# Two bounds of a clipped scan: filled apart on TensorE instead of one widened in place

## The reference

```python
Ad = 1.0 + dt * A                      # (batch, token, 16), just around 1
Bd = Bm * min(norm(xn), 1.0)
def step(h, inputs):
    ad, bd, xt, ct = inputs
    h = clip(h * ad[:, :, None] + bd[:, :, None] * xt[:, None, :], -10.0, 10.0)
    yt = einsum('bd,bdh->bh', ct, h)
    return (h, yt)
```

## Time and profile before

| what | value |
|---|---|
| time, median of 3 runs | 2083.74 us (2082.17 to 2084.46) |
| the profiled execution's own time | 2086.27 us |
| its span in the trace | 2084.4 us, 46452 instructions |
| PE busy | 1916.6 us, 92% |
| POOL busy | 1747.5 us, 84% |
| DVE busy | 1603.2 us, 77% |
| ACT busy | 1377.9 us, 66% |
| TensorE's granted clock, mean | 0.985 of full speed |

### The profile page before, as it was taken

The page is one execution under the profiler, slowest core; times in us unless marked ns, Lnnn a source line. Parts: engine busy times, 40 slices in busy tenths (PEclk is TensorE's granted clock), DMA queues, the critical chain, the costliest instruction groups (busy, mean ns, idle before and its releaser), DMA issues.

```text
span 2084.4 us, 46452 instructions
## 1 busy us (share of the span) xinstructions
PE 1916.6 (92%) x16624; PEld 1441.5 (69%) x16624; DVE 1603.2 (77%) x2045; ACT 1377.9 (66%) x3462; POOL 1747.5 (84%) x1444
## 2 busy tenths in 40 slices
PE   5589999999999999999999999999999999999988
PEld 5467776776776776776677777676777677777665
DVE  3377887878887877887787887787887787887786
ACT  4577666677666667766676766776766676766643
POOL 1388888889888889888889988889988888988886
PEclk9699999999999999999999999999999999999999
DMA  5121212121212121212121112221112121121110
GB/s 175 57 63 44 63 48 63 56 68 44 62 47 63 56 68 49 58 47 63 56 68 52 56 46 64 58 65 53 56 48 64 56 64 57 53 58 53 55 54 16
DMA packets 98437, 122.37 MB, mean 59 GB/s; under 512 B 31072, under 2 KB 68336, under 8 KB 93536
## 3 DMA queue, kind: packets, MB, share of 16 engines
q1 hardware_dynamic: 98208, 119.41, 20.1%
HBM read 62.07 MB, written 9.31 MB: 34 GB/s over the span
## 4 chain that ended last, share of the span: by engine, by line
PE 50%; ACT 18%; issue 15%; DVE 12%; POOL 2%; SPq 2%; DMA 1%; DVEq 0%; ACTq 0%; POOLq 0%
PE ps_y L588 10%; DVE ks L981 7%; PE ps_job L465 7%; PE ps_job L503 7%; PE ps_fill L561 6%; PE ps_fill L552 5%; PE ps_job L478 4%; ACT low L786 4%; ACT tap L744 3%; PE ps_y L568 3%; PE ps_job L472 2%; ACT xh L682 2%; ACT lend L764 1%; ACT gate L676 1%; DVE pf L932 1%
## 5 line engine op out<-in xcount | busy, mean ns | idle before, releaser
L1079 POOL TENSOR_TENSOR prod<-ks,crep 128x512 f32<-128x512 f32 x1024 | 1286.7, 1276 | 159.0 <-DVE ks L981 153.4
L981 DVE TENSOR_TENSOR_SCAN ks<-low,ps_fill 128x512 f32<-128x512 f32 x1024 | 1208.1, 1208 | 255.4 <-PE ps_fill L561 251.6
L786 ACT COPY low<-ps_fill 128x512 f32<-128x512 f32 x1024 | 585.1, 581 | 534.3 <-PE ps_fill L552 534.2
L588 PE MATMUL ps_y<-c_sb,prod 128*128 128x128 f32 x4096 | 610.9, 274 | 2.2 <-POOL prod L1079 1.4
L588 PEld LDWEIGHTS ps_y<-c_sb,prod 128*128 128x128 f32 x4096 | 459.3, 142 | 80.2 <-issue 43.4
L561 PE MATMUL ps_fill<-spans,pick 128*128 128x512 f16 x1024 | 390.3, 381 | 61.8 <-ACT low L786 51.8
L552 PEld LDWEIGHTS ps_fill<-ts,xs 128*128 128x128 f16 x4096 | 315.2, 98 | 174.5 <-issue 8.5
L552 PE MATMUL ps_fill<-ts,xs 128*128 128x128 f16 x4096 | 397.4, 220 | 11.8 <-DVE ks L981 6.0
L744 ACT ACTIVATE tap<-xr,cols_sb 128x128 f32<-128x128 f32 x768 | 251.7, 392 | 0.0
L460 PE MATMUL ps_job<-x,w_in 128*128 128x128 f16 x3072 | 216.5, 222 | 10.3 <-POOL x L1049 7.8
L465 PE MATMUL ps_job<-w_in,x 128*128 128x512 f16 x768 | 203.2, 381 | 21.3 <-ACT gate L676 21.3
(11 more groups left out here) (123 smaller groups left out, 2063.8 us busy)
## 6 DMA issues: line engine op xcount, KB each, us to landing
crep<-c_dram SPq DMA_DIRECT2D x32, 1024.0 KB, 4.8
xs<-xh SPq DMA_DIRECT2D x256, 64.0 KB, 2.0
xs<-xl SPq DMA_DIRECT2D x224, 64.0 KB, 2.0
xf<-in_xT SPq DMA_DIRECT2D x32, 256.0 KB, 2.8
res<-in_x SPq DMA_DIRECT2D x32, 256.0 KB, 2.6
out_dram<-res SPq DMA_DIRECT2D x32, 256.0 KB, 2.1
ts<-tth SPq DMA_DIRECT2D x128, 32.0 KB
ts<-tth SPq DMA_DIRECT2D x128, 31.0 KB
```

Source lines behind the costliest of these rows:

```text
L588: last = mm(ps_y[:, cut], prod[:, (TILES * k + s) % HOLD, e, :], ident, start=False, stop=(u % 4 == 3 and q == 3 and e == QN - 1), is_tran ...
L786: copy(low[:, (TILES * k + s) % RING], ps_fill[:, (TILES * k + s) % RING]).then_inc(sem["low_copied"], 1)
L981: nc.vector.tensor_tensor_scan(ks[:, u % 2, QN * q:QN * (q + 1)].rearrange("d n t -> d (n t)"), low[:, g % RING], ps_fill[:, g % RING], 0. ...
L1079: tt(prod[:, g % HOLD], ks[:, u % 2, part], crep[:, p, part], ALU.mult).then_inc(sem["weighed"], 1)
```

## The change

Each tile's two bounds are made by two fills of the same form. Lower bounds go to two banks (`LOWS`), upper bounds to three (`HIGHS`). The upper fill uses the same weights `xs` and a row stack of its own, `ts[:, p, 1]`, which differs from the lower one in rows 0 and 32 alone (+10/p in place of -10/p). The matmul `widen` with `spans` and `pick` goes. PE runs, in step s, the lower fill of tile s+3 and the upper fill of tile s+2. The slots in `low` become four (`LOWRING`), and ACT's copy now waits for the scan of the tile four back. DVE's scan waits for the copy and for the upper fill.

On SP the stack DMAs run for both row stacks, one stack after the other, so twenty-four in place of twelve; the bounds take four DMAs out and four back in place of three and three; the constant rows of `ts` are loaded four times at the start in place of twice. Two large memsets at the start go. The core of the diff:

```diff
-RING = 5
-AHEAD = 3
+LOWS = 2
+HIGHS = 3
+LOWRING = 4
+AHEAD = (3, 2)
...
-        ts = sb("ts", [P, 2, NSUB, NS * SUB], H)
+        ts = sb("ts", [P, 2, 2, NSUB, NS * SUB], H)
...
-        N_STACK = 16 * (3 * NSUB + NSUB - 1)
-        N_BOUND = 16 * 3
+        N_STACK = 16 * (6 * NSUB + NSUB - 1)
+        N_BOUND = 16 * 4
...
-                    loads.append((ts[96:128, p], carry))
+                    for v in range(2):
+                        loads.append((ts[96:128, p, v], carry))
...
-                    sp.dma_start(r_dram.rearrange("h n t -> n h t"), bnd16[:, :, 1]).then_inc(sem["bound_out"], 16)
...
-                    for jj in range(NSUB):
-                        a = SUB * jj
-                        for r, half in ((0, tth), (SUB, ttl), (2 * SUB, tth)):
+                    for v in range(2):
+                        for jj in range(NSUB):
+                            a = SUB * jj
+                            for r, half in ((0, tth), (SUB, ttl), (2 * SUB, tth)):
+
+                                lead = 0 if r == 2 * SUB else 1
+                                sp.dma_start(ts[r + lead:r + SUB, pn, v, jj],
+                                             half[a + lead:a + SUB].rearrange("s n t -> s (n t)")).then_inc(stack, 16)
...
-            def fill(k, p, s):
+            def fill(k, p, s, v):
...
-                if s == 0:
+                if s == 0 and v == 0:
...
-                since(pe, "scanned", g - RING + 1)
-                o = ps_fill[:, g % RING].rearrange("d (n t) -> d n t", n=QN)
+                if v == 0:
+                    since(pe, "low_copied", g - LOWS + 1)
+                else:
+                    since(pe, "scanned", g - HIGHS + 1)
+                o = ps_fill[:, (g % LOWS, LOWS + g % HIGHS)[v]].rearrange("d (n t) -> d n t", n=QN)
...
-            def widen(k, p, s):
-
-                q = s % NQ
-                pe.wait_ge(sem["low_copied"], TILES * k + s + 1)
-                mm(ps_fill[:, (TILES * k + s) % RING], pick[:], spans[:, p, q * BANK:(q + 1) * BANK], start=False, stop=True,
-                   skip_group_check=True).then_inc(sem["bounded"], 1)
...
+                    ahead(k, p, s + AHEAD[0], 0)
+                    ahead(k, p, s + AHEAD[1], 1)
...
-                    for v, clip in enumerate((-CLIP, 2 * CLIP)):
+                    for v, clip in enumerate((-CLIP, CLIP)):
...
+                    act.wait_ge(sem["low_filled"], TILES * k + s + 1)
+                    since(act, "scanned", TILES * k + s + 1 - LOWRING)
+                    copy(low[:, (TILES * k + s) % LOWRING], ps_fill[:, (TILES * k + s) % LOWS]).then_inc(sem["low_copied"], 1)
...
-                    dve.wait_ge(sem["bounded"], g + 1)
+                    dve.wait_ge(sem["low_copied"], g + 1)
+                    dve.wait_ge(sem["high_filled"], g + 1)
```

More of the change, by code:

```diff
@@ L73 @@
 gw_ready wdt_ready wdt_set sums_ready sums_taken halo_set prep prepared act_prep
-filled low_copied bounded scanned weighed flipped
+low_filled high_filled low_copied scanned weighed flipped
 xr_ready xr_taken xt_ready xt_taken z_ready z_taken zT_ready zT_high zT_taken
@@ L170, in build @@
         xs = sb("xs", [P, 2, NSUB, DI], H)
-        ts = sb("ts", [P, 2, NSUB, NS * SUB], H)
-        low = sb("low", [P, RING, BANK])
+        ts = sb("ts", [P, 2, 2, NSUB, NS * SUB], H)
+        low = sb("low", [P, LOWRING, BANK])
         ks = sb("ks", [P, 2, NS, P])
@@ L333, in body @@
                     xstack, stack = sem[f"xstack_in{pn}"], sem[f"stack_in{pn}"]
-                    since(sp, "filled", TILES * k)
+                    since(sp, "low_filled", TILES * k)
+                    since(sp, "high_filled", TILES * k)
                     sp.wait_ge(sem["xn_done"], j + 1)
@@ L362, in body @@
                     sp.wait_ge(sem["bound_all"], j + 1)
[L363 to L366, removed]
-                    sp.dma_start(r_dram.rearrange("h n t -> n h t"), bnd16[:, :, 1]).then_inc(sem["bound_out"], 16)
+                    for v, bound in enumerate((scratch, r_dram)):
+                        for h in range(2):
+                            sp.dma_start(bound[h].rearrange("j n t -> n j t"),
+                                         bnd16[:, h, v].rearrange("n (j t) -> n j t", j=NSUB)
+                                         ).then_inc(sem["bound_out"], 16)
                     sp.wait_ge(sem["c_out"], 16 * (j + 1))
@@ L375, in body @@
                                      ).then_inc(sem[f"ones_in{pn}"], 16)
[L376 to L383, removed]
-                    sp.wait_ge(sem["tt_done"], 2 * (j + 1))
-                    for jj in range(NSUB):
-                        a = SUB * jj
-                        for r, half in ((0, tth), (SUB, ttl), (2 * SUB, tth)):
-                            lead = 0 if r == 2 * SUB else 1
-                            sp.dma_start(ts[r + lead:r + SUB, pn, jj],
-                                         half[a + lead:a + SUB].rearrange("s n t -> s (n t)")).then_inc(stack, 16)
+                    sp.wait_ge(sem["bound_out"], 64 * (j + 1))
+                    for v, bound in enumerate((scratch, r_dram)):
+                        for h in range(2):
+                            sp.dma_start(ts[SUB * h:SUB * h + 1, pn, v].rearrange("o j c -> o (j c)"),
+                                         bound[h].rearrange("(o j) n t -> o (j n t)", o=1)
+                                         ).then_inc(sem[f"bound_in{pn}"], 16)
+                    sp.wait_ge(sem["tt_done"], 2 * (j + 1))
+                    for v in range(2):
[5 more added lines that the diff above has]
+                                             half[a + lead:a + SUB].rearrange("s n t -> s (n t)")).then_inc(stack, 16)
                     sp.wait_ge(sem["lend_set"], 2 * j + 2)
@@ L620, in body, with ahead @@
                     jobs_at(k, p, 2 * s + 1)
+            def ahead(k, p, s, v):
+                if s < TILES and exists(k, 0):
+                    fill(k, p, s, v)
+                elif s >= TILES and exists(k, 1):
+                    fill(k + 1, 1 - p, s - TILES, v)
             steps(body)
@@ L719, in side @@
                     since(act, "bound_all", k + 1)
-                    since(act, "bound_out", 48 * (k + 1))
-                    for v, clip in enumerate((-CLIP, 2 * CLIP)):
+                    since(act, "bound_out", 64 * (k + 1))
+                    for v, clip in enumerate((-CLIP, CLIP)):
                         act_fn(ad[:, v], pf[:, 0], ACT.Identity, scale=clip).then_inc(sem["bound32"], 1)
@@ L784, in copy_low @@
                 def copy_low(k, s):
-                    act.wait_ge(sem["filled"], TILES * k + s + 1)
-                    copy(low[:, (TILES * k + s) % RING], ps_fill[:, (TILES * k + s) % RING]).then_inc(sem["low_copied"], 1)
+                    act.wait_ge(sem["low_filled"], TILES * k + s + 1)
+                    since(act, "scanned", TILES * k + s + 1 - LOWRING)
+                    copy(low[:, (TILES * k + s) % LOWRING], ps_fill[:, (TILES * k + s) % LOWS]).then_inc(sem["low_copied"], 1)
                 for s in range(TILES):
[L789 to L792, removed]
+                    if s + AHEAD[0] < TILES and exists(k, 0):
+                        copy_low(k, s + AHEAD[0])
+                    elif s + AHEAD[0] >= TILES and exists(k, 1):
+                        copy_low(k + 1, s + AHEAD[0] - TILES)
                     side(k, p, 2 * s)
@@ L807, in _ @@
             nc.vector.memset(unit[:], 1.0)
[L808 to L811, removed]
+            nc.vector.memset(zeros[:], 0.0).then_inc(sem["zeros_set"], 1)
+            dve.wait_ge(sem["zeros_set"], 1)
             nc.vector.memset(halfs[:, 0:1], -0.5)
@@ L981, in scan @@
                     nc.vector.tensor_tensor_scan(ks[:, u % 2, QN * q:QN * (q + 1)].rearrange("d n t -> d (n t)"),
-                                                 low[:, g % RING], ps_fill[:, g % RING], 0.0,
+                                                 low[:, g % LOWRING], ps_fill[:, LOWS + g % HIGHS], 0.0,
                                                  ALU.max, ALU.min).then_inc(sem["scanned"], 1)
@@ L1121 @@
     scratch = nc.dram_tensor("bounds_dram", (2, NSUB, NS, SUB), mybir.dt.float16, kind="Internal").ap()
-    r_dram = nc.dram_tensor("spans_dram", (2, NS, P), mybir.dt.float16, kind="Internal").ap()
+    r_dram = nc.dram_tensor("upper_dram", (2, NSUB, NS, SUB), mybir.dt.float16, kind="Internal").ap()
     c_dram = nc.dram_tensor("c_dram", (1, NS * P), mybir.dt.float32, kind="Internal").ap()
```

16 lines of the change are left out of this document (7 added, 9 removed).

## The result

The changed kernel takes **2400.6 us** (median of 4 runs, 2399.36 to 2401.83), the kernel before 2083.74 in the same session (2082.17 to 2084.46): ratio 1.1522, 95% interval 1.1502 to 1.1542, slower by 317 us. The forecast was 2424, range 2285 to 2490. The profiled execution took 2399.49 us, its span is 2397.7.

The account below looks back on a forecast made before the run. The prediction took SP's stack path to become binding: 27.1 us plus 45.6 from fill to stack, period 72.7 against 62.14, 306 us over 29 chunks. With three open cases, 340 us: 2424 us, range 2285 to 2490.

Parts of the forecast that it names:

- The mechanism: In every chunk PE stands at step 29, 7 to 11 us, for the state behind twenty-four stack DMAs; some 300 us.
- stack path: From a stack's first issue on SP to the next chunk's first fill: 15.6 us unhidden before, 27.1 us forecast.
- The stack, +11.5 us: Twelve more stack DMAs on SP's queue lengthen the path to the first fill by 11.5 us, range 7.3 to 12.1.
- The backlog as the measure, not the issue: Twelve more stack DMAs cost the engines' service time, 11.5 us, not SP's issue time, 7.3 us.
- From fill to stack, 45.6 us: From first fill to the next stack's first issue: 45.6 us, as in chunk 0, where 44.2 follows no wait.
- `lend` landing over 10 us after its issue: Sign in SP's DMA queue: with twenty-four stack DMAs ahead, `lend` lands over 10 us after its issue, not 5.9.
- it was the issue: Rival on SP's queue: twelve more DMAs cost only their issue, 7.3 us; period 68.5, 2290 us, chance 0.11.
- The tighter wait of the upper fill: On PE, the upper fill waits for the scan of s-1, not s-2: zero, bound two scans of 1.21 us a chunk.
- The scan without the widening: On DVE, the scan no longer waits for the widening (251.6 us a launch): no gain, bound 0.2 us a chunk.
- The fills: On PE, a second fill of four matmuls replaces one widening per tile, 0.22 us each: zero.
- the rival that the loads bind: PE pays 98 ns per tile for uncovered weight loads, 2.2 us a chunk: 2487 us, chance 0.06 with anything else slower.
- Hidden, and faster: Rival: transfers stay behind PE's 17.8 us and PE's 61.8 us of waits for the scan's chain go: 2022 us, chance 0.03.

Follow-up runs that it names:

- experiment 3: The changed kernel with twelve DMAs of 31 or 32 rows, each writing both stacks, in place of twenty-four: 2445.45 us, ratio 1.173.
- experiment 4: The kernel before with twelve more stack DMAs a chunk, eight of 32 rows and four of 30, whose data nothing uses: 2281.61 us.
- experiment 6: The changed kernel with twenty-four stack DMAs of 32 rows, one for each stack and block, bounds' rows written after them: 2283.5 us, ratio 1.0958.
- experiment 9: The changed kernel with only the upper fill one step later (tile s+1, not s+2), 31-row transfers kept: 2397.93 us, ratio 1.1511.
- experiment 5: The changed kernel with both stacks brought by twelve DMAs of 32 rows, bounds' rows written after them: 2086.1 us, ratio 1.0009.
- experiment 8: The changed kernel with twelve 32-row DMAs for both stacks, bounds written after, and the upper fill at tile s+1, not s+2: 2068.3 us, ratio 0.9925.
- experiment 7: The kernel before with its twelve stack DMAs at 32 rows and the bounds' rows written after them: 2076.92 us, ratio 0.9965.
- Experiment 2: The changed kernel with one row stack, the second not loaded and both fills reading the first: 2089.59 us, ratio 1.0023.

## Why the prediction was right, and where its sum was off

- **The mechanism** held in each part: a stack path that is no longer hidden, one stand in each chunk, 32 of them, 300.4 us in all (some 300 forecast), 8.81 us in the middle chunk shown (7 to 11).
- **The stack, +11.5 us**: right. Path 26.84 us where 27.1 was forecast; in chunk 0 and for the last stack it grew by 27.25 - 15.80 = 11.45 and by 11.52. The backlog as the measure, not the issue, was confirmed by experiments 3, 4 and 6. The estimate by the Trainium skill's figure of 27 GiB/s an engine ("DMA: Bandwidth & Descriptors", section "Specifications") was about 2338 us; 2400.6 is nearer to the sum from the rows.
- **From fill to stack, 45.6 us: the mis-sized term.** It measured 44.76 in the middle chunk. With the path's 0.26 that makes the period 71.6 in place of 72.7, about 1.06 x 29 = 31 us, and so more than the whole miss on the profiled execution, 2426 against 2399.5 (the first chunk, chunk 0 and the launch's ends were together some 3 us over their terms). The prediction took chunk 0's 45.6 "since PE will have stood longer still". Window tables of whole stretches, from a first fill to the next stack's first issue, show what was off (stretch, us, busy by engine with PE first, granted TensorE clock, DMA): chunk 0 of the kernel before, the change's middle chunk, the change's chunk 0, and a middle chunk of experiment 4.

```profile
155.30:200.88 45.58, 42.55 (x391) 33.24 (x392) 34.52 (x45) 32.22 (x82) 41.40 (x35) 0.96 0.17 45
...
1258.07:1302.83 44.76, 42.60 (x462) 36.30 (x462) 33.90 (x43) 32.18 (x82) 39.05 (x33) 0.96 0.18 52
180.30:226.31 46.01, 43.84 (x462) 37.48 (x462) 34.06 (x43) 32.29 (x82) 39.03 (x33) 0.94 0.16 45
...
1260.50:1306.57 46.07, 43.57 (x391) 34.02 (x392) 34.07 (x43) 32.32 (x82) 39.53 (x34) 0.94 0.19 57
```

  In the first two PE is busy for the same 42.6 us, so what the low clock adds was priced about right. What is gone is idle time of PE inside the stretch: 45.58 - 42.55 = 3.03 us before, 44.76 - 42.60 = 2.16 in the change, and that is the 0.8 us. Experiment 4, with the old fills, has 2.50. So part of it goes with the fills and part with the chunk or the wait before it; which wait each part was is open.

  The longer standing, the reason given, does not decide it either. The clock falls to 0.50 (1.2 GHz) while PE stands and returns after it works again, here in the change after 8.81 us of standing:

```profile
1324.00:1329.60 5.60, 0.00 (x0) 0.00 (x0) 0.00 (x0) 0.00 (x0) 1.60 (x2) 0.50 0.59 162
1329.67:1333.00 3.33, 3.33 (x24) 3.27 (x25) 1.73 (x2) 2.19 (x5) 0.00 (x0) 0.50 0.27 81
1333.00:1335.00 2.00, 2.00 (x28) 1.98 (x27) 1.56 (x2) 1.86 (x4) 1.19 (x1) 1.00 0.04 8
```

  How much work falls at 0.50 differs. The change's chunk 0, after 14.08 us of standing, is 1.25 us longer than the middle chunk, at the same idle time (2.17). Experiment 3, whose fills are the change's, has both lengths in two chunks one after the other:

```profile
1209.02 1.01 PE L556 MATMUL ps_fill<-ts,xs 128*128 128x128 f16 x8 [9.95 <-DMA xs<-h]
1282.87 1.01 PE L556 MATMUL ps_fill<-ts,xs 128*128 128x128 f16 x8 [9.81 <-DMA xs<-h]
...
1209.02:1214.90 5.88, 5.88 (x41) 5.73 (x42) 2.95 (x3) 3.91 (x7) 1.75 (x1) 0.51 0.19 50
1282.87:1286.50 3.63, 3.63 (x26) 3.57 (x27) 2.04 (x2) 2.49 (x5) 0.00 (x0) 0.50 0.22 78
1209.02:1255.06 46.04, 43.84 (x462) 37.48 (x462) 34.02 (x43) 32.30 (x82) 39.07 (x33) 0.94 0.18 50
1282.87:1327.88 45.01, 42.81 (x462) 36.49 (x462) 33.94 (x43) 32.22 (x82) 39.10 (x33) 0.96 0.18 52
```

  After nearly the same stand, 5.9 us of work ran at 0.50 in one and 3.6 in the other; the 2.25 us between them cost 1.03, about what half speed would (1.1). What chooses between the two is not shown. With the change's period at 71.64, most of its chunks must have had the short one; with the long one in each, the period would have been near 26.84 + 46.0 = 72.9 (an estimate), and the forecast would have looked better for no merit of its own.
- **`lend` landing over 10 us after its issue: wrong**, it lands after 6.0 (5.9 before), by the change's list of DMA issues:

```profile
lend<-lend SPq DMA_DIRECT2D x32, 64.0 KB, 6.0
```

  "With twenty-four the queue only grows" was the false step: from the twelfth issue on SP is held, so the queue stays where it was and the time shows on SP, as L391's 25% of the chain. By the prediction's own test, "if the landing of `lend` stays near 6 us and the period is near 68, it was the issue", the period decides: 71.6.
- **The tighter wait of the upper fill, taken as zero**: right in this kernel (experiment 9). Of the two reasons given, that PE gets it back at step 29 is borne out only in part: the standing grew by 3.8 us where 56 us of waiting for the scan went. That DVE is not waiting for PE there doesn't hold by itself: with the stack path hidden, the step is worth 17.8 us (experiments 5 and 8), 0.56 a chunk. That is well under the bound of two scans.
- **The scan without the widening, taken as zero, at most 0.2 us a chunk**: hidden here. With the stack path hidden, all that differs between experiments 7 and 8 is worth 8.6 us, 0.27 a chunk, a little over the bound; the scan's part in it was not measured apart.
- **The fills** kept their 0.22 us for four: PE's timeline at full clock has eight in 1319.69 - 1319.24 = 0.45 us.

```profile
1319.24 0.61 PE L556 MATMUL ps_fill<-ts,xs 128*128 128x128 f16 x8
1319.69 0.61 PE L585 MATMUL ps_y<-c_sb,prod 128*128 128x128 f32 x4
```

  Experiment 2 puts all of the change but the transfers at some 5 us, so the rival that the loads bind falls. The Trainium skill's 81 ns a matmul ("TensorE: Matmul & The Clock Gate", section "Back-to-back issue gap") is not seen here; these rows have 56.
- **Hidden, and faster**: its condition, twelve more DMAs under 0.18 us each, was not met, but its second half is real. Where the second stack costs no more issues and no queue (experiment 8), the time is 0.75% under the kernel before, not the rival's 3%. Of that 0.35% is the 32-row stack (experiment 7) and 0.4% the change's fills.

## What to carry to other kernels

Read a serial DMA queue as a path of its own, with its slack: here 3 us of slack stood against a 12-transfer addition, and no busy share of an engine showed it. Look at a transfer's rows before its bytes: writing one row too many and repairing it afterwards was worth 117 us where a 31-row form was on the path (experiment 6), and 314 together with half the issues (experiment 5). And a wait priced at zero because something longer covers it can come back when the cover goes: with the stack mended, the same step was worth 18 us.

## What the hardware showed that was not expected

- SP is held at the issue when its transfers are behind. In the change an issue goes from 0.62 us (first eleven) to 0.99 (last thirteen); in experiment 3, with transfers of twice the bytes, the fifth takes 3.02 us. In experiments 5 and 6, with 32 rows, nearly all issues keep to about 0.6 us. The backlog seen by `lend` stayed at 6.0 - 2.0 = 4 us in the change, as before it.
- A transfer of 32 rows that writes each row to two places (64 KB) landed after 2.0 us in experiment 5, and its issue cost 0.60 to 0.65 us, no more than for one place: twelve such issues took 7.79 us.
- The work that ran at the low clock after a stand of PE did not follow the length of the stand: 3.3 us after 8.81, 3.6 after 9.81, but 5.9 after 9.95.
